# Two accumulating DMAs add and fold the squares of a phase-mixer layer in place of GpSimd

## The chip, the cores and the metric
One core of a Trainium2 chip runs the whole program. The metric is the device time of one execution in microseconds (us). The kernel before took 1530.54, 1533.1 and 1534.26 us in three runs; the median is 1533.1 us.

## What is computed
The input is 16 sequences of 1024 rows by 256 numbers. A layer norm comes first, then a phase mixer, then a second layer norm and a feed-forward part with ternary weights. What matters here, in the reference's own names (cut):

```python
omega = einsum('bsd,ed->bse', x, W_omega) + b_omega
phi = cumsum(omega * exp(log_scale) / sqrt(position), axis=1)
cm_real, cm_imag = x * cos(phi), x * sin(phi)
mem_real = cumsum(cm_real, axis=1) / position
mem_imag = cumsum(cm_imag, axis=1) / position
ret_real = mem_real * cos(phi) + mem_imag * sin(phi)
ret_imag = mem_imag * cos(phi) - mem_real * sin(phi)
context = concatenate([cm_real, cm_imag, ret_real, ret_imag], axis=-1)
h = layernorm(context, ln_gamma, ln_beta)          # needs mean and variance of 1024 numbers a row
h = gelu(h @ W1.T + b1) @ W2.T + b2
x = x + normed_x + h                               # then the feed-forward part, relu between two matmuls
```

The variance of the context needs the sum of its squares. Because cos and sin squared add to one, the squares of ret_real and ret_imag add to those of mem_real and mem_imag; the kernel therefore squares the two memories.

## The kernel before, in words
The rows are cut into 32 chunks of 512 rows, two to a sequence. Inside a chunk, features lie on the 128 partitions (two blocks, KD = 2) and rows along the free axis (CH = 512), so that the cumulative sums are scans along the free axis. A step of the main loop works on several chunks at once: `now` is in the feed-forward part, `nxt` in the two matmuls of the mixer, `ahead` (two chunks on) in the phase, memory and square part, `far` (three on) in its first layer norm, and `before` (one back) hands out its result. The loop is unrolled. Each engine has its own hand-written order of the work of a step, and semaphores join them.

The squares of the chunk `ahead` go this way. ScalarE squares mem_real into the tile `sqr` (`square_real`, L652) and mem_imag into the tile `turn` (`square_imag`, L661), in the middle of its relu work. GpSimd then waits for both and for `cl_done[3]`, which VectorE's last `context_lo` (L1332) gives, adds `turn` to `sqr` (L535, 128x1024 float32) and adds the second feature block to the first (the fold, L537, 128x512). At the start of the next step ScalarE rounds the folded sum to float16 (`sums_hi`, L656), and GpSimd takes the rest (`square_lo`, L544). TensorE sums over the partitions (L945) in the middle of the mixer's first matmul (L966). After L656, ScalarE's order goes on with `base_scaled` (L581), `whole_turns` (L608, which writes the tile `turn` again and so waits for `q2_done`), `output` (L614) and the sine (L620). VectorE's `fraction` (L1250) waits for L608 and opens VectorE's step; its order then is the first layer norm's statistics (L1170), the two products and scans of the memories (L1263, L1271, L1257, L1285), the second layer norm's lower half (`second_lo`, L1392), the scaling of the hidden rows (L1356, four blocks), and so on to `context_lo`, `mixer_residual` (L1368), the phase scans (`phase_sums`, L1237) and the second statistics (L1375 to L1386).

SyncE issues four DMA transposes of `rows2` (L438) when `second_lo` is done; TensorE's feed-forward matmul (L987) reads what they write. Four more (L446) turn the first norm's rows for `omega` (L926). SyncE also loads `x_rows` (L450) and stores the residual rows to the output (L453).

GpSimd's order in a step is: `base_bias` (DMA, L490), `inverse_std_2` (L502), `square_lo` (L544), `inverse_std_1` (L478), `x1_bias` (DMA, L494), `inverse_std_context` (L507), `product_imag_sin` (L551), `retrieve` (two accumulating DMAs, L483 and L486, which add the second product of ret_real and ret_imag to the first), `output_sum` (L498, an accumulating DMA of the chunk `before` onto the output in DRAM), and `square_sums` (L535, L537). All of GpSimd's DMAs go through one software queue, q0.

Of the kernel before, what the change touches and what calls it, by code (L numbers as in the profile page):

```python
# [17 lines left out]
ALU = mybir.AluOpType  # L18
# [25 lines left out]
def phase_mixer_layer(nc, x, w_omega, b_omega, log_scale, ln_gamma, ln_beta, w1, b1, w2, b2,  # L44
# [17 lines left out]
    with ctx:  # L62
        def sb(name, shape, dt=F32):
            return ctx.enter_context(nc.sbuf_tensor(name, shape, dt))

        def sem(name):
            return ctx.enter_context(nc.semaphore(name))
# [76 lines left out]
        turn = sb("turn", [P, KD, CH])  # L144
# [13 lines left out]
        sqr = sb("sqr", [P, KD, CH])  # L158
# [108 lines left out]
        cl_done = [sem(f"cl_done{i}") for i in range(4)]  # L267
        sqr_done, sqi_done, q2_done, q_done = sem("sqr_done"), sem("sqi_done"), sem("q2_done"), sem("q_done")
# [61 lines left out]
        def wait(eng, s, value):  # L330
            if not isinstance(value, int) or value > 0:
                eng.wait_ge(s, value)

        def need(eng, s, c, back=0):

            wait(eng, s, c.counts.value(1, c.more + 1 - back))
# [5 lines left out]
        def need_sum(eng, s, c, back=0):  # L342

            wait(eng, s, c.counts.value(16, 16 * (c.more + 1 - back)))
# [18 lines left out]
        def run(eng, step, first):  # L363

            for s in range(first, CHUNKS):
                step(Step(Counts(eng, s - s % 2), s % 2))
# [36 lines left out]
        def first_chunks(eng):  # L403

            return [Chunk(Counts(eng, 0), more) for more in range(2)]

        def prepared(eng):

            eng.wait_ge(p_lo, len(W1_GROUPS))
            eng.wait_ge(p_scales, 3)  # L410
            eng.wait_ge(p_thr, 1)
            eng.wait_ge(p_tab, 16)
# [53 lines left out]
        @block.gpsimd  # L466
        def _(pool):
            pool.memset(ident[:, :], 0.0).then_inc(p_zero, 1)
            pool.wait_ge(p_zero, 1)
            pool.affine_select(out=ident[:, :], in_=ident[:, :], compare_op=ALU.not_equal, fill=1.0, base=0,  # L470
                               pattern=[[-1, P]], channel_multiplier=1).then_inc(p_ident, 1)
            pool.memset(e_base[:, :], 2.718281828459045).then_inc(p_const, 1)
            pool.memset(minus_half[:, :], -0.5).then_inc(p_const, 1)
            pool.memset(one_half[:, :], 0.5).then_inc(p_const, 1)
            pool.wait_ge(p_const, 3)
            def inverse_std_1(c):
                need(pool, ve1_done, c)
                pool.tensor_tensor(rs1[:, c.b], ve1[:, :], minus_half[:, :], ALU.pow).then_inc(rs1_done, 1)  # L478

            def retrieve(c):  # L480
                need(pool, ra_done, c)
                need(pool, qa_done, c)
                pool.dma_start(rr[:, :, :], qa[:, :, :], accum_op=ALU.add).then_inc(rr_done, 16)  # L483
                need(pool, rb_done, c)
                need(pool, qb_done, c)
                pool.dma_start(ri[:, :, :], qb[:, :, :], accum_op=ALU.add).then_inc(ri_done, 16)  # L486

            def base_bias(c):
                need(pool, scaled_done, c)
                pool.dma_start(base[:, c.b], b2_rows, accum_op=ALU.add).then_inc(base_biased[c.b], 16)  # L490

            def x1_bias(c):
                need(pool, xs2_done, c)
                pool.dma_start(x1[:, c.b], f_b2_rows, accum_op=ALU.add).then_inc(x1_biased[c.b], 16)  # L494

            def output_sum(c):
                need(pool, out_done, c)
                pool.dma_start(out_v[c.index], x1[:, c.b], accum_op=ALU.add).then_inc(added[c.b], 16)  # L498

            def inverse_std_2(c):  # L500
                need(pool, ve2_done, c)
                pool.tensor_tensor(rs2[:, :], ve2[:, :], minus_half[:, :], ALU.pow).then_inc(rs2_done, 1)  # L502

            def inverse_std_context(c):
                need(pool, cve_done, c)
                need(pool, spread_done, c, 1)
                pool.tensor_tensor(crs[:, :], cve[:, :], minus_half[:, :], ALU.pow).then_inc(crs_done, 1)  # L507

            def step(s):
                before, now, nxt, ahead, far = s.chunk(-1), s.chunk(0), s.chunk(1), s.chunk(2), s.chunk(3)  # L510
                if ahead:
                    base_bias(ahead)
                if now:
                    inverse_std_2(now)
                if nxt:
                    square_lo(nxt, ahead)
                if far:
                    inverse_std_1(far)
                if now:
                    x1_bias(now)  # L520
                if nxt:
                    inverse_std_context(nxt)
                if ahead:
                    product_imag_sin(ahead)
                    retrieve(ahead)
                if before:
                    output_sum(before)
                if ahead:
                    square_sums(ahead)

            def square_sums(c):
                need(pool, sqr_done, c)
                need(pool, sqi_done, c)
                need(pool, cl_done[3], c)
                pool.tensor_tensor(sqr[:, :, :], sqr[:, :, :], turn[:, :, :], ALU.add).then_inc(q2_done, 1)  # L535
                need(pool, q2_done, c)
                pool.tensor_tensor(sqr[:, 0], sqr[:, 0], sqr[:, 1], ALU.add).then_inc(q_done, 1)  # L537

            def square_lo(c, after):
                if after:  # L540
                    need(pool, frac_done, after)
                need(pool, q_done, c)
                need(pool, qh_done, c)
                pool.tensor_tensor(q_lo, sqr[:, 0], q_hi, ALU.subtract).then_inc(ql_done, 1)  # L544

            def product_imag_sin(c):
                need(pool, mi_done, c)
                need(pool, sin_done, c)
                need(pool, sumr_done, c)
                need_sum(pool, rr_done, c, 1)  # L550
                pool.tensor_tensor(qa[:, :, :], mi[:, :, :], sn[:, :, :], ALU.mult).then_inc(qa_done, 1)  # L551

            first, second = first_chunks(pool)
            pool.wait_ge(p_om, 32)
            pool.tensor_tensor(exp_ls[:, :], e_base[:, :], lscale[:, :], ALU.pow).then_inc(p_exp, 1)
            inverse_std_1(first)
            pool.wait_ge(p_root, 1)
            pool.tensor_tensor(mags_all[:, 1:2], mags_all[:, 1:2], one_half[:, :], ALU.pow).then_inc(p_max, 1)
            inverse_std_1(second)
            retrieve(first)  # L560
            square_sums(first)
            pool.wait_ge(p_bias, 32)
            base_bias(first)
            prepared(pool)
            run(pool, step, -1)

        @block.scalar
        def _(act):
# [35 lines left out]

            def whole_turns(c):
                need(act, y_done, c)
                need(act, q2_done, c, 1)
                act.activation(turn[:, :, :], ph[:, :, :], ACT.Identity, bias=rounder[:, 0:1]).then_inc(turn_done, 1)  # L608

            def output(c):  # L610
# [41 lines left out]
                act.activation(sqr[:, :, :], mr[:, :, :], ACT.Square, scale=SQUARE_SCALE).then_inc(sqr_done, 1)  # L652

            def sums_hi(c):
                need(act, q_done, c)
                act.copy(q_hi, sqr[:, 0]).then_inc(qh_done, 1)  # L656

            def square_imag(c):
# [78 lines left out]
            def step(s):  # L737
# [10 lines left out]
                if not now:  # L748
                    whole_turns(ahead)
                if nxt:  # L750
                    sums_hi(nxt)
                if ahead:
                    base_scaled(ahead)
                if now and ahead:
                    whole_turns(ahead)
# [114 lines left out]
            for i, (s, w) in enumerate(((p_fw1, fw1_in), (p_fw2, fw2_in))):  # L870
                act.wait_ge(s, 16)
                if i:
                    act.wait_ge(p_abs, i)
                act.activation(dump, w.rearrange("p m d -> p (m d)"), ACT.Abs,
                               accum_out=abs_sums[:, i:i + 1]).then_inc(p_abs, 1)
            act.wait_ge(p_abs, 2)
            whole_turns(first)
            act.wait_ge(p_scales, 2)
            group_hi(1)
# [809 lines left out]
```

## Time and profile before

| | us |
|---|---|
| median of three runs | 1533.1 |
| lowest, highest | 1530.54, 1534.26 |
| the profiled execution | 1533.96 |
| its span, first to last instruction | 1532.2 |
| TensorE busy in it | 1470.5 (96%) |
| VectorE busy | 1438.2 (94%) |
| ScalarE busy | 1253.4 (82%) |
| GpSimd busy | 616.9 (40%) |

The granted TensorE clock averages 0.991 of full speed over the span. Busy time is a union of instruction times; TensorE's matmuls are pipelined and overlap in it. "PE" is TensorE, "DVE" VectorE, "ACT" ScalarE, "POOL" GpSimd and "SP" SyncE; L535 is line 535 of the kernel. Times inside the execution are counted from the span's start.

### The profile page before, as it was taken

Reading aid. Unit: us, or ns where it says so; the run is one execution under the profiler, and the core shown is the slowest. Engines: PE = TensorE matmul, PEld = TensorE weight load, DVE = VectorE, ACT = ScalarE, POOL = GpSimd, SP = SyncE. Lnnn points to the kernel's source line nnn. Section 1 sums busy time; section 2 is a strip of 40 time slices with the busy share of each in tenths; the row PEclk is TensorE's granted clock in tenths of the full one; section 3 lists DMA queues with packets and bytes.
Section 4 is the critical chain, followed back from the end, with each engine's and each line's share of the span. In section 5 each row is a group of like instructions: output and inputs, shape, how many; then the busy total and the mean of one; then the engine's idle time right before and its main releaser. Section 6 shows DMA issues by size and latency. Waiting matters only on the chain.

```text
span 1532.2 us, 29929 instructions
## 1 busy us (share of the span) xinstructions
PE 1470.5 (96%) x10685; PEld 878.0 (57%) x10685; DVE 1438.2 (94%) x2325; ACT 1253.4 (82%) x1773; POOL 616.9 (40%) x393
## 2 busy tenths in 40 slices
PE   3779999999999999999999999999999999999998
PEld 2445566656555665555665655566565566555556
DVE  7999999999999999999999999999999999989954
ACT  6768888888988888988888898888888788888756
POOL 1333444433354443444444334444344444334331
PEclk9899999999999999999999999999999999999999
DMA  6325545555645655654555564455565455555452
GB/s 219 67 58 111 102 80 109 108 111 113 123 76 100 111 104 111 124 107 79 105 111 110 111 125 94 83 111 103 109 125 109 73 109 111 110 111 101 73 90 42
DMA packets 231427, 158.20 MB, mean 103 GB/s; under 512 B 138608, under 2 KB 221552, under 8 KB 231280
## 3 DMA queue, kind: packets, MB, share of 16 engines
q0 software_dynamic: 59376, 83.37, 34.3%
q1 hardware_dynamic: 170272, 69.25, 18.4%
q10 hardware_dynamic: 1632, 3.67, 0.7%
q8 instruction: 86, 1.41, 0.4%
q14 instruction: 61, 0.50, 0.1%
HBM read 24.13 MB, written 33.03 MB: 37 GB/s over the span
## 4 chain that ended last, share of the span: by engine, by line
DVE 35%; PE 24%; issue 14%; ACT 12%; POOL 7%; DMA 4%; SPq 2%; DVEq 1%; ACTq 0%; POOLq 0%
PE ps L966 11%; DVE arena L1332 5%; POOL sqr L535 4%; DVE arena L1400 4%; PE ps L1000 4%; PE ps L987 4%; POOL sqr L537 3%; PE ps L1021 3%; ACT xs L601 3%; DVE mr L1285 3%; ACT base L581 3%; DVE arena L1361 2%; DVE bn L1170 2%; DVE arena L1356 2%; DVE qb L1316 2%
## 5 line engine op out<-in xcount | busy, mean ns | idle before, releaser
L966 PE MATMUL ps<-arena,w_hi 128*128 128x512 f16 x2048 | 609.2, 379 | 3.0 <-DVE arena L1332 1.6
L966 PE MATMUL ps<-arena,w_lo 128*128 128x512 f16 x1024 | 388.3, 379 | 0.0
L966 PEld LDWEIGHTS ps<-arena,w_hi 128*128 128x128 f16 x2048 | 197.5, 98 | 224.2 <-issue 2.0
L987 PE MATMUL ps<-turned,fw_t 128*128 128x512 f16 x1024 | 250.6, 380 | 8.6 <-DMA turned<-rows 4.1
L1000 PE MATMUL ps<-fw_t,arena 128*128 128x256 f16 x2048 | 255.0, 273 | 1.9 <-DVE arena L1400 1.9
L1000 PEld LDWEIGHTS ps<-fw_t,arena 128*128 128x128 f16 x2048 | 197.8, 97 | 63.8 <-issue 16.7
L704 ACT ACTIVATE arena<-ps,relu_bias,relu_scale 128x512 f32<-128x512 f32 x256 | 197.0, 769 | 24.8 <-PE ps L987 24.4
L535 POOL TENSOR_TENSOR sqr<-sqr,turn 128x1024 f32<-128x1024 f32 x32 | 84.3, 2635 | 323.3 <-DVE arena L1332 323.3
L1400 DVE TENSOR_TENSOR arena<-arena 128x512 f16<-128x512 f32 x256 | 172.0, 681 | 19.5 <-ACT arena L713 17.5
L1021 PE MATMUL ps<-w_hi,arena 128*128 128x256 f16 x1024 | 172.9, 273 | 0.3 <-issue 0.3
L966 PEld LDWEIGHTS ps<-arena,w_lo 128*128 128x128 f16 x1024 | 100.0, 98 | 121.0
L987 PEld LDWEIGHTS ps<-turned,fw_t 128*128 128x128 f16 x1024 | 97.5, 98 | 109.4 <-DVE arena L1356 14.6
L713 ACT CAST arena<-arena 128x512 f16<-128x512 f32 x256 | 154.5, 615 | 4.3
L1021 PE MATMUL ps<-w_lo,arena 128*128 128x256 f16 x512 | 139.6, 273 | 0.0
L656 ACT CAST sqr<-sqr 128x512 f16<-128x512 f32 x32 | 19.8, 617 | 128.4 <-POOL sqr L537 128.4
L483 POOL DMA_DIRECT2D rr<-qa x32 | 29.5, 921 | 203.4 <-DVE rr L1322 203.4
L551 POOL TENSOR_TENSOR qa<-mi,sn 128x1024 f32<-128x1024 f32 x31 | 73.3, 2364 | 86.5 <-DVE mr L1285 86.5
L1021 PEld LDWEIGHTS ps<-w_hi,arena 128*128 128x128 f16 x1024 | 100.0, 98 | 12.6 <-issue 0.7
L670 ACT ACTIVATE arena<-arena,b_full,z_down 128x512 f32<-128x512 f32 x128 | 96.9, 804 | 10.9 <-DVE arena L1356 10.8
L1361 DVE SCALAR_TENSOR_TENSOR arena<-arena,up 128x512 f16<-128x512 f32 x128 | 92.0, 741 | 0.0
L1356 DVE TENSOR_TENSOR arena<-ps,rb 128x512 f32<-128x512 f32 x128 | 82.0, 682 | 8.9 <-ACT rb L666 6.2
L676 ACT ACTIVATE arena<-arena,up 128x512 f16<-128x512 f32 x128 | 88.1, 713 | 1.0
(189 smaller groups left out, 2850.4 us busy)
## 6 DMA issues: line engine op xcount, KB each, us to landing
x_rows<-in_L_attn_x SPq DMA_DIRECT2D x32, 512.0 KB, 6.5
rr<-qa POOLq DMA_DIRECT2D x32, 512.0 KB, 6.2
ri<-qb POOLq DMA_DIRECT2D x32, 512.0 KB, 9.0
base<-bias_rows POOLq DMA_DIRECT2D x32, 512.0 KB, 5.5
x<-bias_rows POOLq DMA_DIRECT2D x32, 512.0 KB, 5.5
out<-x SPq DMA_DIRECT2D x31, 512.0 KB, 7.6
out<-x POOLq DMA_DIRECT2D x31, 512.0 KB, 11.2
arena<-in_L_attn_W ACTq DMA_DIRECT2D x1, 2048.0 KB, 11.8
```

The source lines that it names most:

```text
L535: pool.tensor_tensor(sqr[:, :, :], sqr[:, :, :], turn[:, :, :], ALU.add).then_inc(q2_done, 1)
L670: act.activation(z[:, m], z[:, m], ACT.Gelu, scale=z_down[:, 0:1], bias=b1_full[:, m:m + 1])\
L676: act.activation(gh[:, m], z[:, m], ACT.Copy, scale=up[:, 3:4]).then_inc(gh_done[m], 1)
L704: act.activation(rf[:, m % SLOTS], ps[:, 4 + m % KE], ACT.Relu, scale=relu_scale[:, 0:1], bias=relu_bias[:, m:m + 1]).then_inc(relu_done, 1)
L713: act.copy(rh[:, m % SLOTS], rf[:, m % SLOTS]).then_inc(rh_done, 1)
L966: last = pe.matmul(ps[:, 4 + m], w[:, k, m * P:(m + 1) * P], a[:, c.b, k], start=(i == 0), stop=(i == len(passes) - 1))
L987: last = pe.matmul(ps[:, 4 + m % KE], fw1_t[:, k, m * P:(m + 1) * P], a[:, k], start=(i == 0), stop=(i == len(passes) - 1))
L1000: last = pe.matmul(ps_rows_a[:, j], a[:, m % SLOTS, j * P:(j + 1) * P], fw2_t[:, m], start=(m == 0 and j % 2 == 0 and a is rh), stop=(m == ...
L1021: last = pe.matmul(rows[:, j], a[:, m, j * P:(j + 1) * P], w[:, m], start=(i == 0), stop=(i == len(passes) - 1))
L1356: dve.tensor_tensor(z[:, m], ps[:, 4 + m], rb[:, :], ALU.mult).then_inc(z_done[m], 1)
L1361: dve.scalar_tensor_tensor(out=gl[:, m], in0=z[:, m], scalar=up[:, 3:4], in1=gh[:, m], op0=ALU.mult, op1=ALU.subtract).then_inc(gl_done[m], 1)
L1400: dve.tensor_tensor(rl[:, m % SLOTS], rf[:, m % SLOTS], rh[:, m % SLOTS], ALU.subtract)\
```

## The change
GpSimd's addition L535 and its fold L537 become two accumulating DMAs, issued by GpSimd on its software queue; the second waits until the first has landed. The wait for `cl_done[3]` goes. The readers of the two sums count DMA landings (16 to a DMA) in place of one. `output_sum`, the DMA that adds a chunk's result to the output, moves from behind `retrieve` to ahead of `product_imag_sin`.

```diff
--- before.py
+++ after.py
@@ step of GpSimd @@
                 if nxt:
                     inverse_std_context(nxt)
+                if before:
+                    output_sum(before)
                 if ahead:
                     product_imag_sin(ahead)
                     retrieve(ahead)
-                if before:
-                    output_sum(before)
                 if ahead:
                     square_sums(ahead)
 
             def square_sums(c):
                 need(pool, sqr_done, c)
                 need(pool, sqi_done, c)
-                need(pool, cl_done[3], c)
-                pool.tensor_tensor(sqr[:, :, :], sqr[:, :, :], turn[:, :, :], ALU.add).then_inc(q2_done, 1)
-                need(pool, q2_done, c)
-                pool.tensor_tensor(sqr[:, 0], sqr[:, 0], sqr[:, 1], ALU.add).then_inc(q_done, 1)
+                pool.dma_start(sqr[:, :, :], turn[:, :, :], accum_op=ALU.add).then_inc(q2_done, 16)
+                need_sum(pool, q2_done, c)
+                pool.dma_start(sqr[:, 0], sqr[:, 1], accum_op=ALU.add).then_inc(q_done, 16)
 
             def square_lo(c, after):
                 if after:
                     need(pool, frac_done, after)
-                need(pool, q_done, c)
+                need_sum(pool, q_done, c)
@@ whole_turns of ScalarE @@
-                need(act, q2_done, c, 1)
+                need_sum(act, q2_done, c, 1)
@@ sums_hi of ScalarE @@
-                need(act, q_done, c)
+                need_sum(act, q_done, c)
```

## Rows read from the trace of the kernel before
**Rows 1.** The page: busy time of the engines, and the chain by engine.
```profile
PE 1470.5 (96%) x10685; PEld 878.0 (57%) x10685; DVE 1438.2 (94%) x2325; ACT 1253.4 (82%) x1773; POOL 616.9 (40%) x393
DVE 35%; PE 24%; issue 14%; ACT 12%; POOL 7%; DMA 4%; SPq 2%; DVEq 1%; ACTq 0%; POOLq 0%
```
**Rows 2.** Windows: stretch, length, busy PE, PEld, DVE, ACT, POOL, clock, DMA share, GB/s.
```profile
697.60:742.50 44.90, 44.65 (x328) 26.69 (x327) 43.77 (x70) 38.20 (x54) 19.39 (x13) 1.00 0.56 107
715.00:720.00 5.00, 5.00 (x26) 2.29 (x24) 4.97 (x8) 4.57 (x7) 2.37 (x1) 1.00 0.40 81
```
**Rows 3.** TensorE's waits from 120 to 1440 us: total, times, longest.
```profile
PE ps L987 <- DMA turned<-rows: 4.1, 7, 1.0
PE ps L987 <- DVE arena L1356: 3.6, 10, 0.7
PE ps L926 <- DMA turned<-xs: 3.0, 1, 3.0
```
**Rows 4.** GpSimd's timeline in one step: start us, us, engine, line.
```profile
712.00 1.93 POOL L507 TENSOR_TENSOR crs<-cve,minus_half 128x4 f32<-128x4 f32 x1 [1.91 <-DVE cve L1349]
716.78 2.37 POOL L551 TENSOR_TENSOR qa<-mi,sn 128x1024 f32<-128x1024 f32 x1 [2.85 <-DVE mr L1285]
...
727.14 0.85 POOL L486 DMA_DIRECT2D ri<-qb  x1 [1.09 <-DVE qb L1316]
727.68 1.63 POOL L498 DMA_DIRECT2D out<-x  x1
739.40 2.64 POOL L535 TENSOR_TENSOR sqr<-sqr,turn 128x1024 f32<-128x1024 f32 x1 [10.09 <-DVE arena L1332]
742.12 2.06 POOL L537 TENSOR_TENSOR sqr<-sqr 128x512 f32<-128x512 f32 x1
```
**Rows 5.** ScalarE's timeline over the same step and into the next.
```profile
699.24 0.62 ACT L656 CAST sqr<-sqr 128x512 f16<-128x512 f32 x1 [4.18 <-POOL sqr L537]
...
731.26 1.06 ACT L661 ACTIVATE turn<-mi 128x1024 f32<-128x1024 f32 x1
...
744.22 0.62 ACT L656 CAST sqr<-sqr 128x512 f16<-128x512 f32 x1 [3.66 <-POOL sqr L537]
...
746.72 1.13 ACT L608 ACTIVATE turn<-ph,rounder 128x1024 f32<-128x1024 f32 x1
```
**Rows 6.** VectorE's timeline: the phase scans, and the first work of the next step.
```profile
741.11 4.15 DVE L1237 TENSOR_TENSOR_SCAN ph<-ones,ph 128x512 f32<-128x512 f32 x2
...
747.89 1.22 DVE L1250 SCALAR_TENSOR_TENSOR ph<-turn,ph 128x1024 f32<-128x1024 f32 x1
```
**Rows 7.** One line's instructions, L1285: a scan of the same shape, min/median/max ns.
```profile
L1285 DVE TENSOR_TENSOR_SCAN mr<-ones,mr_carry,cmr x32: 1251/1264/1276, 83.7 to 1443.1; 128x512 f32<-128x512 f32 x32
```
**Rows 8.** DMA issues between 724.5 and 740 us: KB, us from issue to landing.
```profile
ri<-qb POOLq DMA_DIRECT2D x1, 512.0 KB, 9.5
out<-x POOLq DMA_DIRECT2D x1, 512.0 KB, 12.1
```
**Rows 9.** DMA issues between 50 and 60 us, with no other traffic.
```profile
rr<-qa POOLq DMA_DIRECT2D x1, 512.0 KB, 4.7
```
**Rows 10.** SyncE's timeline: the four transposes L438, mid-run and in the last steps.
```profile
713.13 5.35 SPq L438 DMA_TRANSPOSE turned<-rows  x4
1477.21 7.46 SPq L438 DMA_TRANSPOSE turned<-rows  x4
```
**Rows 11.** DMA issues, landings of such transposes: from 713 us; the one at 1483.4.
```profile
turned<-rows SPq DMA_TRANSPOSE x4, 2.5
turned<-rows SPq DMA_TRANSPOSE x1, 3.2
```
**Rows 12.** TensorE's timeline: the first feed-forward matmuls of the step.
```profile
720.15 2.75 PE L987 MATMUL ps<-turned,fw_t 128*128 128x512 f16 x12
```
**Rows 13.** The chain that ended last, before the loop: start us, us, what.
```profile
65.48 2.23 DVE ph L1237
```
**Rows 14.** TensorE's waits from 1440 us to the end.
```profile
PE ps L1000 <- DVE arena L1400: 1.9, 2, 1.6
```

## The prediction
> **What bounds the kernel now.** I read the page first. TensorE is busy 96% of the span and VectorE 94%, and yet the chain that ended last runs through every engine, 7% of it GpSimd's [rows 1]. So two limits lie close together, and the step has to be read as a cycle. The windows show one step: TensorE is busy 44.65 of 44.90 us [rows 2]. Its waits over the whole loop come to 10.7 us: 3.6 for VectorE's scaled hidden rows (10 times), 4.1 for the turned rows (7 times), and one of 3.0 [rows 3]. Some 29 steps lie there, so TensorE alone would want about 44.85 us a step.
>
> The timelines give the other limit. L656 starts at 699.24 and again at 744.22, a period of 44.98 [rows 5]. From L656 ScalarE leads to L608, that releases VectorE's L1250, VectorE runs almost without a gap (43.77 of 44.90 us [rows 2]) until L1332 releases GpSimd's L535 at 739.40; L535 and L537 end at 744.18 [rows 4], and the circle closes at 744.22. It is a cycle of 44.98 against TensorE's 44.85. Even if this cycle became much shorter, TensorE would keep the loop where it is. **The prize is small**: what TensorE waits for.
>
> **The change, part by part.**
>
> L535 and L537 removed. They cost 4.78 us of the cycle [rows 4] and something on VectorE: the two phase scans L1237 beside them take 4.15 us [rows 6], where the scans of the same shape at another place take 1.26 each [rows 7], so 2.5 for two. That is 1.6 to 1.9 us of VectorE's time a step. In the loop it is slack. Before the loop it is on the chain: L1237 has 2.23 us there and its fellow about as much [rows 13], against 1.26 each. **Term 1: -1.9 us**, once.
>
> The first DMA. It may start when L661 has ended, at 731.26 + 1.06 = 732.32 [rows 5]; the wait for L1332 is gone. No row shows this DMA. One of its kind and size, rr<-qa, lands 4.7 us after its issue with nothing beside it [rows 9]; ri<-qb in traffic takes 9.5 [rows 8]. Here the same queue still holds ri<-qb, issued at 727.14 and landed at 727.14 + 9.5 = 736.6. The result's DMA, which followed it, landed at 727.68 + 12.1 = 739.8, so 512 KB behind another 512 KB cost 3.2 more [rows 4, 8]. That place in the queue is now free and the squares take it: 736.6 + 3.2 = 739.8. The bounds are 737.0 (4.7 after the issue) and 741.9 (9.5 after it).
>
> The second DMA, the fold. GpSimd waits for the first; behind that wait stands nothing that could run, as the next in its order, L490, needs ScalarE's next step. Half the bytes: 4.7 less half of 3.2 is 3.1 us, so q_done is at 739.8 + 0.1 + 3.1 = 743.0, against 744.18 now. With the bounds of the first DMA, and 2.5 and 4.7 for the fold, it lies between 739.6 and 746.7. I take 743.0, as the queue's own rows are nearest. L656, L608 and L1250 then come 1.2 us earlier against TensorE. VectorE can follow: it saves up to 1.9 at the scans. Its hidden rows (L1356) are ready 1.2 earlier, more than the longest such wait (0.7 [rows 3]). **Term 2: -3.6 us.** I bound it by 0 and by all of the loop's waits, 10.7.
>
> The Trainium skill, "DMA: Bandwidth & Descriptors", section "Anatomy of one DMA", gives 2.0 us fixed and the bytes over 436 GB/s for a DMA of GpSimd's; that would be an estimate of 3.2 and 2.6 us, 5.8 for the two, and it also says that the fixed part is mostly the receipt of the last write, so two in a row pay it twice. By it q_done would be at 738.2 and the sum the same, since VectorE's own work then ends the wait. The row of 4.7 us for 512 KB disagrees with 3.2, and I go by the row.
>
> The result's DMA moved. It goes past GpSimd's L551 and the two accumulating DMAs of `retrieve`. GpSimd is free from 712.00 + 1.93 = 713.93 until L551 at 716.78, and the issue takes 1.63 [rows 4]: it fits into the 2.85 us of waiting, at no cost. If that cover were gone, L551 and with it rr<-qa would be up to 1.6 later, and ScalarE has 3.66 us of waiting at the step's end [rows 5] to take it. Its data wait for `out_done`, done long before. `mixer_residual` needs it landed, and it now lands some 13 us earlier. But its transfer now meets SyncE's transposes L438. These are issued from 713.13 to 718.48 [rows 10], the last at about 717.3, and land 2.5 later [rows 11], at 719.8; TensorE takes them at 720.15 [rows 12]. The slack is 0.35 us, and 1.55 with the 1.2 won above. The result's 3.2 us of transfer begin about 715.6. From 715 to 720 the DMA engines are 0.40 busy [rows 2], so up to 719.1 some 3.5 x 0.6 = 2.1 us are free, and 3.2 - 2.1 = 1.1 us of delay is left for the last transpose. 1.55 - 1.1 = 0.45 us is about today's slack, so today's 4.1 us of waits stay. **Term 3: 0**, between -4.1 and what the first rival says.
>
> The last steps. TensorE waits 1.9 us for L1400 after 1440 us [rows 14], because VectorE comes late with its queue of work; it comes about 1.2 earlier, and I count half. **Term 4: -0.9 us**, between 0 and -1.9. The changed semaphore counts and the lost wait for L1332 on GpSimd cost nothing by themselves.
>
> Sum: -1.9 - 3.6 + 0 - 0.9 = -6.4 us. Against the profiled execution, 1533.96, that is 1527.6; against the median, which is 0.9 lower, **1526.7 us**.
>
> **The rivals.**
>
> *Slower: the transposes starve behind the result's DMA.* One place in the trace has transposes beside a 512 KB DMA of GpSimd's, the group at 1477.21: its four issues take 7.46 us in place of 5.35 [rows 10], and the last lands after 3.2 in place of 2.5 [rows 11]. That is 2.1 + 0.7 = 2.8 us of delay, not 1.1. It decides from 1.55 on. At 2.8 TensorE waits 1.25 us a step, the step is 46.1, and 29 x (46.1 - 44.98) = 32, less term 1: about 1563 us. At 2.0 it is +0.45 a step, some +7 in all. For it: that row. Against it: there, the DMA's data came first and whole; here the first two transposes are ahead. The Trainium skill, same page, section "Queues, rings and completion order", says that an engine takes turns between queues, a packet at a time. By this rule a transpose would wait for little in front of it, and this rival would not come; the group at 1477.21 speaks against the rule's being enough.
>
> *Slower: the two DMAs in a row are late.* If the first takes ri<-qb's 9.5 and the fold a full 4.7, q_done is at 746.7, 2.5 later than now, on a cycle that has no slack: 29 x 2.5 = 73 us, near 1604. It needs traffic at 737 to 742, where none is now.
>
> *No change.* VectorE's gain goes into waiting for L608, the waits for hidden rows turn into as many for turned rows (term 3 at +3 in place of 0), and some 3 us are left: 1530 to 1534.
>
> *That the change does not do what it says* could only be if the DMAs were held by something else on q0. Nothing of GpSimd's is issued there between 729.3 and 744 [rows 4].
>
> **How the numbers follow.** A measurement of this kernel tells about 0.3%, 4.6 us, from no change. The forecast and what is better than it, faster by over 4.6: 0.45. No change, and the part of the forecast that falls short: 0.31. Starved transposes 0.16 and late DMAs 0.08, together slower: 0.24. The likeliest case's own range is 1519 to 1531; its lower end is all of the waits, 10.7 + 1.9 + 1.9 = 14.5 below 1533.1. The range of 8 in 10 reaches up to a transposes' delay between 2.0 and 2.8: 1519 to 1550.
>
> **What would show each step.** GpSimd: two DMA issues at about 732.4 and 739.9 of this step in place of L535 and L537, the new L656 at about 743.0, and its DMA `out<-x` issued from 713.9. VectorE: L1237 at 2.4 to 2.5 us for two, and L1250 waiting up to 0.7 us more for L608. TensorE: waits for L1356 near 0, waits for the turned rows near 4, a step of 44.85 to 44.9. The last transpose should land 3.6 after its issue, against 2.5. The forecast is wrong if the landing of the first square DMA is after 741, or if the turned rows' waits exceed 10 us in the loop; it is too careful if both kinds of waits vanish.

## The result, and the profile after

The changed kernel takes 1541.3 us (median of 5, 1539.47 to 1546.26), the kernel before in the same comparison 1533.1. The ratio is 1.0064, with a 95% interval of 1.0043 to 1.0085: **8 us slower**, where I had forecast 6.4 us faster. The range, 1519 to 1550, holds it; the direction is wrong. It is the side of the first rival, at the lower end of its price. The profiled execution has a span of 1538.0 us, 5.8 longer than the one before.

The changed kernel's page, busy times and the chain by engine (lines of the kernel from L498 to L534 move by up to 3; later ones are one lower than before):

```profile
PE 1471.5 (96%) x10685; PEld 877.5 (57%) x10685; DVE 1373.0 (89%) x2325; ACT 1254.1 (82%) x1773; POOL 522.0 (34%) x393
PE 59%; DMA 11%; ACT 10%; SPq 7%; DVE 7%; issue 5%; POOL 0%; ACTq 0%; DVEq 0%; POOLq 0%
```

Against [rows 1], GpSimd has lost 95 us and VectorE 65. GpSimd is gone from the chain, and VectorE's share of it has fallen from 35% to 7%. TensorE's has grown from 24% to 59%, that of the DMAs from 4% to 11%, and that of SyncE's queue, which issues the transposes, from 2% to 7%. TensorE's waits between 120 and 1440 us, which answer to [rows 3], are now of one kind:

```profile
PE ps L986 <- DMA turned<-rows: 16.7, 19, 2.1
```

The 3.6 us for VectorE's hidden rows are gone, as term 2 had it, and so is the single wait of 3.0, which it had left standing. The wait for the turned rows has gone from 4.1 to 16.7, so all of TensorE's waits in the loop from 10.7 to 16.7. SyncE's timeline and GpSimd's over one step say why (compare [rows 10, 4]):

```profile
760.07 7.03 SPq L438 DMA_TRANSPOSE turned<-rows  x4
```
```profile
760.85 1.28 POOL L498 DMA_DIRECT2D out<-x  x1
763.61 2.35 POOL L550 TENSOR_TENSOR qa<-mi,sn 128x1024 f32<-128x1024 f32 x1 [1.48 <-DVE mr L1284]
...
782.17 0.86 POOL L534 DMA_DIRECT2D sqr<-turn  x1 [4.99 <-ACT turn L660]
788.69 0.85 POOL L536 DMA_DIRECT2D sqr<-sqr  x1 [5.67 <-DMA sqr<-turn]
```

The result's DMA is issued 0.8 us after the first transpose. The four issues take 7.03 us in place of 5.35. Over the run, a transpose of this group lands 4.8 us after its issue (median of 124), against 2.5. The trace also records every packet, the pieces in which a DMA moves its data; each transpose has 512. The last packet of the four comes 8.5 us after the first issue (median of the loop's steps), against 5.9 before, and the last landing comes at 9.2 against 6.6. Both are **2.6 us later**. In the step above, no data packet of the transposes starts between 762.3 and 765.0, while 256 of the result's 512 do. That is one of the harder steps: the longest such stop is 1.5 us in the median step, and 0.6 in the kernel before. The chain of this step shows how the delay becomes the period (start us, us, what; cut):

```profile
757.85 0.21 PE ps L944 x8
758.09 0.16 DVE cmu L1336
...
758.76 1.24 DVE rows L1391
...
760.07 1.83 SPq L438
...
763.28 2.50 SPq L438
...
765.83 3.57 DMA turned<-rows
...
769.45 1.05 PE ps L986 x4
```

TensorE's own sums of the context (L944) release VectorE's variance; right behind it stands `second_lo` (L1391), which releases the transposes, and these release TensorE's feed-forward matmul. It is a loop that begins and ends on TensorE. However early the squares are ready, this part cannot start before L944. VectorE's waits in the changed kernel, 120 to 1440 us, have a kind that the kernel before has once in this stretch, with 0.4 us (total, times, longest):

```profile
DVE cmu L1336 <- PE ps L944: 14.0, 20, 0.9
```

The first transpose is issued 2.0 us after the end of L944's sums, against 3.6 before (medians of the loop). So the start has come 1.6 us forward, though the squares are ready 2.5 us sooner, and it can come no further; what a transpose is late beyond the slack is paid in full.

### The profile page after: what moved, and what is told of

Read it like the earlier page. It is cut to its first block, busy times and chain, and to the rows that moved or that the text cites. A ratio compares the mean times of both kernels' runs of the same rounds, so it can differ in the third digit from the quotient of the medians.

```text
span 1538.0 us, 29929 instructions
## 1 busy us (share of the span) xinstructions
PE 1471.5 (96%) x10685; PEld 877.5 (57%) x10685; DVE 1373.0 (89%) x2325; ACT 1254.1 (82%) x1773; POOL 522.0 (34%) x393
## 4 chain that ended last, share of the span: by engine, by line
PE 59%; DMA 11%; ACT 10%; SPq 7%; DVE 7%; issue 5%; POOL 0%; ACTq 0%; DVEq 0%; POOLq 0%
PE ps L965 22%; PE ps L986 11%; PE ps L999 11%; PE ps L1020 8%; SPq L438 7%; DMA turned<-rows 5%; PE ps L925 4%; DMA sqr<-turn 3%; ACT arena L703 3%; PE ps L938 2%; DMA sqr<-sqr 2%; DVE rows L1391 2%; ACT base L580 1%; ACT xs L600 1%; DVE bn L1169 1%
## 5 line engine op out<-in xcount | busy, mean ns | idle before, releaser
L986 PE MATMUL ps<-turned,fw_t 128*128 128x512 f16 x1024 | 247.4, 379 | 17.7 <-DMA turned<-rows 17.3
L999 PE MATMUL ps<-fw_t,arena 128*128 128x256 f16 x2048 | 254.8, 272 | 1.9 <-DVE arena L1399 1.9
L999 PEld LDWEIGHTS ps<-fw_t,arena 128*128 128x128 f16 x2048 | 195.8, 97 | 69.3 <-issue 30.5
L490 POOL DMA_DIRECT2D base<-bias_rows x32 | 42.2, 1317 | 169.5 <-ACT base L580 169.5
L655 ACT CAST sqr<-sqr 128x512 f16<-128x512 f32 x32 | 19.8, 618 | 93.4 <-DMA sqr<-sqr 93.4
```

Source lines behind the costliest of these rows:

```text
L986: last = pe.matmul(ps[:, 4 + m % KE], fw1_t[:, k, m * P:(m + 1) * P], a[:, k], start=(i == 0), stop=(i == len(passes) - 1))
L999: last = pe.matmul(ps_rows_a[:, j], a[:, m % SLOTS, j * P:(j + 1) * P], fw2_t[:, m], start=(m == 0 and j % 2 == 0 and a is rh), stop=(m == ...
```

## The experiments

All comparisons are with the kernel before on the same chip. e5 and e9 leave out part of what they should add to the output; they are there for their times alone.

| run | us | ratio (95%) |
|---|---|---|
| e1, squares by DMA, result's DMA at its old place | 1566.9 | 1.0213 (1.018 to 1.0247) |
| e2, result's DMA moved, GpSimd adds | 1594.6 | 1.0396 (1.0359 to 1.0432) |
| e3, squares by DMA, result's DMA early | 1518.8 | 0.9902 (0.9871 to 0.9933) |
| e4, result's DMA behind GpSimd's product | 1534.2 | 1.0012 (0.9987 to 1.0038) |
| e5, a quarter of the result's DMA, in place | 1519.1 | 0.9906 (0.9874 to 0.9937) |
| e6, result's DMA early, GpSimd adds | 1534.2 | 1.0009 (0.999 to 1.0029) |
| e7, e3 with the wait for cl_done[3] kept | 1663.2 | 1.085 (1.0813 to 1.0887) |
| e8, e3 with GpSimd's adds, no such wait | 1546.9 | 1.0094 (1.0064 to 1.0125) |
| e9, half of the result's DMA, in place | 1519.5 | 0.9896 (0.9864 to 0.9929) |

**e1 and e2 take the change apart.** e1 undoes the move:

```diff
                 if nxt:
                     inverse_std_context(nxt)
-                if before:
-                    output_sum(before)
                 if ahead:
                     product_imag_sin(ahead)
                     retrieve(ahead)
+                if before:
+                    output_sum(before)
```

> The changed kernel with the result's DMA back behind the two retrieving DMAs; the squares stay with the two accumulating DMAs. Theory A (the transposes L438 wait behind the result's DMA on the same 16 engines, and this alone made the kernel slower): the transposes' issues take 5.1 to 5.4 us for four again and land after 2.5, TensorE's waits for turned rows fall from 17.3 us to 4 or less. But the result's DMA (3.3 us of transfer) now stands ahead of the squares on q0, so the fold lands about 3.2 later and L655 starts 11.5 to 14 us after the square L660 ends, against 8.6 to 10.4 in the changed kernel. The stretch from L655 to the end of L660 was 33.1 in the kernel before and cannot shrink much, so the step is 33.1 + 13 = 46 us: 1560 to 1575 us. Rival B (the order of the DMAs on q0 does not matter, only the transposes do): TensorE's waits vanish and the kernel is at 1525 to 1530.

Measured: 1566.9. GpSimd's timeline, the two square DMAs behind the result's:

```profile
740.47 1.64 POOL L498 DMA_DIRECT2D out<-x  x1
745.27 0.87 POOL L534 DMA_DIRECT2D sqr<-turn  x1 [3.16 <-ACT turn L660]
```

The first square DMA now lands 9.1 us after its issue (median), against 5.2 in the changed kernel. From the end of ScalarE's second square to its L655 it is 13.5 us (median of the loop), where the changed kernel has 9.3 and the kernel before 11.8. The transposes land after 2.5 us again, with their last packet at 5.9, but TensorE still waits 7.5 us for them in the loop, where I had 4 or less, and it waits for VectorE (11.0 us) and GpSimd (15.3) besides. Theory A's two halves hold, its price too; B is out.

e2 is the kernel before with `output_sum` moved behind `inverse_std_context`, and nothing else.

> The kernel before with the result's DMA moved ahead of GpSimd's product alone; GpSimd adds and folds the squares as before. Theory A: the last transpose is 2.4 us later after the first one's issue, as in the changed kernel (8.2 to 8.5 us to its last packet, against 6.1), and without the 1.2 to 1.6 us that the squares' DMAs win for VectorE's start the slack of 0.35 us is all there is: TensorE waits about 1.5 to 2.1 us a step, the loop is 45 to 60 us longer, 1575 to 1590 us. Rival B (the squares' DMAs made the kernel slower, the moved DMA is harmless): 1530 to 1535 us, transposes at 2.5.

Measured: 1594.6, a little above the expected range, and TensorE's waits:

```profile
PE ps L987 <- DMA turned<-rows: 51.8, 26, 3.2
```

A transpose of the first four lands after 4.7 us (median), and their last packet comes 8.5 us after the first issue, as in the changed kernel. Not all of the price is waiting. The first transpose's issue stays 3.6 us behind TensorE's sums here, so the waits are long, and behind eight of them, of 2.0 to 2.9 us each, the granted clock is 0.50 (1.2 GHz) for 3.4 us. One such stretch, in the form of [rows 2]:

```profile
654.10:657.50 3.40, 3.40 (x10) 1.18 (x8) 1.53 (x3) 2.86 (x5) 0.00 (x0) 0.50 0.52 104
```

Ten matmuls of 128x512 start in it; at full clock, twelve take 2.75 us [rows 12]. Half of 3.4 us, eight times, is an estimate of 14 us of the 60. So the move alone costs 60 us, and each part of the change alone is a loss: the squares' DMAs 33 us where the result's stands ahead of them, the move 60 us where VectorE starts late. Together they lose only 8, because the faster squares start VectorE sooner and pay for most of the move's delay.

**e3, e6 and e4 move the DMA elsewhere.** e3 is the changed kernel with

```diff
                 if nxt:
                     square_lo(nxt, ahead)
+                if before:
+                    output_sum(before)
                 if far:
                     inverse_std_1(far)
...
                     inverse_std_context(nxt)
-                if before:
-                    output_sum(before)
```

> The changed kernel with the result's DMA issued earlier, right behind square_lo and ahead of GpSimd's first inverse_std (about 4 us sooner), so that its 3.3 us of transfer end before the third transpose; the x1_bias DMA goes behind it. Theory A: the transposes wait less than 1 us (last packet 6.1 to 7 us after the first issue), TensorE's waits for turned rows fall below 5 us, and the gain that I had predicted shows: 1524 to 1530 us. Against it: inverse_std_1 is 1.3 to 1.6 us later and the bias DMA behind it may now be the one that meets the transposes; then 1532 to 1540. Rival B (the squares' DMAs are what costs): no change against the changed kernel, 1538 to 1543.

Measured: 1518.8, **15 us faster than the kernel before** and 22 faster than the changed one. Theory A's mechanism holds, but it gains 5 us more than its range allowed. The first window is the kernel before, the second e3, both from 120 to 1440 us:

```profile
120.00:1440.00 1320.00, 1308.83 (x9600) 778.47 (x9599) 1281.44 (x2046) 1112.05 (x1572) 561.18 (x349) 1.00 0.56 104
```
```profile
120.00:1440.00 1320.00, 1319.86 (x9658) 786.46 (x9655) 1233.63 (x2059) 1127.60 (x1587) 465.17 (x353) 1.00 0.66 123
```

TensorE is busy for all of the loop but 0.14 us. The transposes land after 2.5 us (median), with their last packet at 6.2, although GpSimd's bias DMA now goes out behind the result's. No wait of TensorE is left in the loop for another order to win; of the kernels measured with a whole result, this is the one to keep.

e6 has e3's order, but GpSimd's adds of the kernel before.

> The kernel before with the result's DMA moved early alone (behind square_lo); GpSimd adds and folds the squares as before, behind its wait for cl_done[3]. Theory A (the gain of the early variant, 14 us, is that of the squares' way, since the result's DMA was never in anyone's way at its old place): the cycle through L535 and L537 stays at 44.98 us, 1530 to 1536 us. Rival D (the early variant gained by clearing the result's DMA out of the traffic of 725 to 739, and the squares' DMAs are only neutral): 1519 to 1525 us.

Measured: 1534.2, no change. Theory A holds, and D is out: the early place wins nothing by itself. The whole gain of e3 comes by the squares.

e4 is the changed kernel with `output_sum` between `product_imag_sin` and `retrieve`.

> The changed kernel with the result's DMA issued behind GpSimd's product and ahead of the two retrieving DMAs. It then leaves the four transposes L438 alone and meets the second four (L446, for omega). Theory A (a transpose waits for all bytes that stand in front of it on the engines): L438's last packet is back at 6.1 us or less behind the first issue, L446's goes from 5.9 to 8.3. The second four had 0.8 us of slack in the kernel before and some 1.4 more in this one, so TensorE waits 0 to 0.5 us a step, for turned<-xs in place of turned<-rows: 1518 to 1534 us. Rival (the delay is special to L438, whose matmul comes first): L446 stays at 5.9 and the time is that of the early variant, 1519.

Measured: 1534.2, with single runs from 1526.6 to 1542.4. SyncE's timeline and TensorE's waits:

```profile
715.02 5.34 SPq L438 DMA_TRANSPOSE turned<-rows  x4
722.47 6.35 SPq L446 DMA_TRANSPOSE turned<-xs  x4
```
```profile
PE ps L926 <- DMA turned<-xs: 12.2, 8, 4.2
```

The delay has gone over to the other four transposes (landing 3.7 us, against 2.5), whose last packet is at 7.1, against 5.9. I had expected 8.3 of it. The first four are nearly undisturbed, with their last packet at 6.3. The rival is out; the price is that of the upper end, by few but long waits.

**e5 and e9 shrink the DMA in place.**

```diff
-                pool.dma_start(out_v[c.index], x1[:, c.b], accum_op=ALU.add).then_inc(added[c.b], 16)
+                pool.dma_start(out_v[c.index][:, 0:1], x1[:, c.b, 0:1], accum_op=ALU.add).then_inc(added[c.b], 16)
```

> The changed kernel with the result's DMA cut to the first quarter of its rows (128 packets in place of 512, 0.8 us of transfer in place of 3.3); three quarters of the feed-forward part's contribution to the output are left out. Everything else stands, the place of the DMA too. Theory A: the transposes' delay follows the bytes in front of them, under 0.8 us in place of 2.4, TensorE's waits for turned rows fall below 4 us, 1523 to 1530 us. Rival C (a transpose waits for the DMA's being in flight, whatever its size): the delay stays above 1.5 us and the time within 3 us of the changed kernel's 1541.

e9 has 0:2 in place of 0:1.

> The changed kernel with the result's DMA cut to half of its rows (256 packets, 1.65 us of transfer); the other half of the feed-forward part's contribution to the output is left out. A third point between the whole (last packet of the transposes L438 at 8.2 to 8.5 us behind their first issue, 1541 us) and the quarter (5.9 to 6.8 us, 1519). Theory A1 (a transpose stands behind every byte that is queued ahead of it, and SyncE's next issue behind it): the delay over the undisturbed 5.9 is 1.0 to 1.6 us, which the 1.55 us of slack still cover: 1518 to 1524 us. Theory A2 (my reckoning in the prediction: the result's transfer fills the gaps between the transposes, of which there are 2.1 us): no delay at all, last packet at 6.1 or less.

Measured: 1519.1 and 1519.5, both as fast as e3; for e5 that is 4 us below the range of theory A. The transposes' last packet comes at 6.5 and 6.6 us, against 5.9 undisturbed and 8.5 with the whole. So C is out: the size decides. But a quarter and a half delay alike, 0.6 to 0.7 us, and the second half adds 1.9, more than its own 1.65 us of transfer. Neither A1 (1.0 to 1.6 for the half) nor A2 (nothing) has it right. That the gaps between the transposes take up a small transfer and none of a larger one is a reading of these three points, not shown by them. The times cannot part a quarter from a half, as both delays lie inside the slack.

**e7 and e8 ask what the squares' DMAs win by.** e7 is e3 with `need(pool, cl_done[3], c)` kept ahead of the first of them.

> The early variant with GpSimd's wait for cl_done[3] kept in front of the first square DMA. Theory: two DMAs in a row take 4.7 + 0.1 + 3.3 us, 3.4 more than GpSimd's 4.8, and pay only because they may start 7 us sooner. Started at the old place they end 3.3 us later than GpSimd's adds did: the step becomes 44.98 + 3.3 = 48.3, 1620 to 1635 us. Rival (what gained is the freed VectorE, not the earlier start): no slower than 1535.

Measured: 1663.2, some 30 us above the expected range. GpSimd's timeline, one step:

```profile
701.18 0.85 POOL L535 DMA_DIRECT2D sqr<-turn  x1 [11.81 <-DVE arena L1332]
705.98 0.85 POOL L537 DMA_DIRECT2D sqr<-sqr  x1 [3.94 <-DMA sqr<-turn]
```

From ScalarE's square to its rounding it is now 16.0 us (median), 4.2 more than in the kernel before, where I had 3.3, and the period of the loop is 49.5 us. The DMAs themselves cost the 3.3 more that I had reckoned. Another 0.6 lies ahead of them: they start 7.6 us behind the square, where GpSimd's add started 7.0 behind it. TensorE waits for GpSimd almost every step here, and its granted clock averages 0.961 over the span, against 0.991 before. That the lower clock is what makes the wait for `cl_done[3]` end later is likely, and not shown. The DMAs are slower than GpSimd's adds; the earlier start is what pays.

e8 is e6 without `need(pool, cl_done[3], c)`.

> The early variant with GpSimd's own add and fold in place of the two DMAs, but without the wait for cl_done[3], so that they start right behind ScalarE's second square. It tells the DMAs from the earlier start. Theory E (the start is all; GpSimd's adds would do as well): the fold ends near 738 to 741, off the cycle, and the kernel is at 1518 to 1524 us as with the DMAs. Theory F (GpSimd and VectorE hold each other up: the phase scans beside the adds took 2.1 us each in place of 1.2 to 1.3, and beside relu_lo and context_lo the adds now cost VectorE 2 to 5 us a step just where TensorE waits for it): VectorE's L1399 or L1331 take longer, TensorE waits for L1399, 1530 to 1560 us.

Measured: 1546.9. The timeline of GpSimd, and VectorE's `relu_lo` by line, in e8:

```profile
697.03 4.07 POOL L534 TENSOR_TENSOR sqr<-sqr,turn 128x1024 f32<-128x1024 f32 x1 [4.60 <-ACT turn L660]
```
```profile
L1399 DVE TENSOR_TENSOR arena<-arena 128x512 f16<-128x512 f32 x256 | 205.0, 810 | 43.7 <-ACT arena L712 40.1
```
```profile
PE ps L999 <- DVE arena L1399: 12.5, 29, 0.4
```

The fold is done early enough: 6.6 us from square to rounding. But GpSimd's add takes 4.07 us (3.91 on average) in place of 2.64 [rows 4], and `relu_lo` takes 810 ns on average; in e6, which differs by the wait alone, it is 683. One `context_lo` a step (L1331, of ret_real) takes 2.04 us in place of 1.21. TensorE waits for `relu_lo` once in each of 29 steps, 12.5 us in all, and e8 is 12.7 us slower than e6. Theory E falls, F holds: GpSimd's adds can start early only beside VectorE's subtractions, and there both are slowed. The Trainium skill, "SBUF — State Buffer", section "Who interferes with whom", says that a VectorE instruction with two inputs in SBUF contends with a GpSimd instruction that reads SBUF; these runs agree, as `relu_lo`, `context_lo` and the add all read two tiles of SBUF.

## Why the prediction was wrong, point by point

*What bounds the kernel.* The cycle was read right: e7 and e1 lengthen it and pay it step by step. The **prize was too small** in my sum. I took the waits for hidden rows alone, 3.6 us, and left those for turned rows where they were; e3 shows that all of the loop's waits could go. Its period is 44.79 us, measured between the first and last L655 of the loop, against 45.36, which is 0.57 x 28 = 16 us. I had compared 44.85 with one smooth step of 44.98, and the average step was longer than that. The waits on record are 10.7 of these 16 us. The one of 3.0 was followed by 3.4 us at a granted clock of 0.50, from 1363.8 us, which cost up to 1.7 more (an estimate, half of 3.4). The other 4 us lie in what the profile counts as TensorE's busy time, and no run says why.

*Term 1*, -1.9: right, at 2.15. The second L607, before the loop, starts at 65.74 in place of 67.89 us, and the phase scans take 2.33 us for two in the loop, against 4.15 [rows 6].

*Term 2*: the mechanism was right. I had 10.7 us from the square to the rounding; it is 9.3 (median). The first DMA lands 5.2 us after its issue, against my 7.4, because ri<-qb in front of it lands 7.9 us after its own, in place of the 9.5 of my row. What shortens ri<-qb is not shown. That the result's DMA no longer follows it can be a part at most, as ri<-qb still takes 8.7 in e6.

*Term 3*, 0: **the step that failed**. It set 1.1 us of delay for the last transpose against 1.55 us of slack, so that no new wait was left. The delay is 2.6. It comes in two parts (medians of the loop). The last transpose lands 3.6 us after its own issue in place of 2.5, which is the 1.1 of my sum and the very sign that I had named. But I had let the issues run as before, and they stretch: the four take 6.7 us in place of 5.1. That the first part came out to the tenth is partly luck, for it was reckoned from gaps of 715 to 720 that the transfer was to fill, with the issues on time. The slack assumed that the transposes start earlier by what the squares win; they do so only until L944 on TensorE caps it. From the end of those sums TensorE has 10.7 us of its own work up to its feed-forward matmul, and in the kernel before the last transpose landed 10.2 us behind them (medians). That is a slack of 0.45 us, and 2.0 with the 1.6 won; without the cap the squares' 2.5 us would have made it 2.95, enough for the whole delay. The 2.6 less 2.0 leave 0.6 us a step, and the measured waits, 16.7 us over 29 steps, are 0.58. My sign for being wrong, more than 10 us of these waits, came. The wrong choice was to take a sharing that no row showed over the one row that had both together, the group at 1477.21 with its 2.8 us [rows 10, 11]; I had that row and gave it 0.16. Its price was too high: worked out as there, a delay of 2.6 us would have cost some +25, against the measured +8, as the squares had won more slack than the 1.2 us that I had. That the range holds the time is luck: it comes of its width, not of a right sum.

I had weighed there what the Trainium skill, "DMA: Bandwidth & Descriptors", section "Queues, rings and completion order", says of turns between queues at packets. The packet records show such turns in one place and none in another. In the step of the changed kernel that begins its transposes at 714.10, 362 packets of SyncE's queue go beside 127 of GpSimd's from 717.0 to 719.0, and then 1 beside 195 from 719.3 to 720.3. The rule alone does not give the delay, and the measurement decides.

*Term 4*, -0.9: wrong. TensorE's waits for L999 are 1.9 us, as before, in the changed kernel and in e3.

*The other rivals.* Late square DMAs did not come by themselves; e1 and e7 are what they would have been. The issue of the moved DMA did fit into GpSimd's waiting, at no cost.

What stays open: whether the transposes stop because their packets queue behind the others on each engine, or because SyncE's next issue is held until the last one moves. In the steps shown, the issues stretch from 5.35 to 7.03 us and the landings too, so both may be at work; no run parts them. In the step at 760.07 the first transpose's packets start 1.2 us behind its issue, the second's 3.1 us behind theirs, and the records do not say where they stood until then.

## What to carry to other kernels

When a DMA is moved, look at what else uses the DMA engines in the few us behind its new place, and whether a matmul waits for that; if one row of the trace shows the two together, its delay goes into the forecast. Here, a place 4 us earlier on the same queue turned +8 us into -15. And a slow way off a busy engine may beat a fast way on it, if it can start sooner: here, two DMAs of together 8.5 us won over 4.8 us of GpSimd's adds. A wait of TensorE can cost more than its length: look at the granted clock behind the long ones.

## What the runs showed of the hardware that I had not expected

- Four DMA transposes beside a 512 KB accumulating DMA of GpSimd's: the last packet at 8.5 us in place of 5.9; beside 256 or 128 KB of it, 6.6 and 6.5.
- An accumulating DMA within SBUF takes 4.5 us for 512 KB where the one ahead of it on its queue has landed (e7, median), 5.2 where that is still under way (changed kernel), and 3.3 for 256 KB.
- In e2, eight waits of TensorE of 2.0 to 2.9 us were each followed by 3.4 us at a granted clock of 0.50.
- GpSimd's 128x1024 add beside VectorE's work on two SBUF operands: 4.07 us (3.91 on average), against 2.64 beside the scans, which were themselves slowed from 1.2 to 2.1.
